# Attention scores from two 12-bit parts in the two halves of the array's rows, in a block of attention and routed experts

## The reference, cut to what matters

```python
def attn(x, Wq, Wk, Wv):                      # x (8, 512, 128), 16 heads of 8 columns; Wk, Wv (8, 128): one k and v for all heads
    q = (x @ Wq.T).reshape(B, S, NH, DK).transpose(0, 2, 1, 3)
    k, v = x @ Wk.T, x @ Wv.T
    dist = softmax(einsum('bhqd,bkd->bhqk', q, k) * DK ** -0.5)
    return einsum('bhqk,bkd->bhqd', dist, v).transpose(0, 2, 1, 3).reshape(B, S, 128)

mod = (silu(c) @ wmod)                         # six rows of 128 for each batch: sa, ca, ga, sb, cb, gb
h = layernorm(x) * (1 + ca) + sa
x = x + ga * attn(h, Wq, Wk, Wv)
h = layernorm(x) * (1 + cb) + sb
x = x + gb * ffn(h)                            # 8 experts of 128 -> 512 -> 128 with gelu, the best 2 for each token
```

## Time and profile before

| what | value |
|---|---|
| runs | 617.99, 621.27 and 1950.61 us, median 621.27 |
| span of the profiled execution, first to last instruction | 616.6 us |
| its own time with what lies around the span | not given; the nearest run is 617.99, 1.4 above the span |
| busy share of the span | PE 90%, DVE 81%, ACT 72%, POOL 52% |
| chain that ended last | PE 66%, DVE 17%, ACT 5% |
| granted TensorE clock | 0.977 of 2.4 GHz over the span |

### The profile page before, as it was taken

One profiled execution on the slowest core, in us unless ns is written; L12 is line 12 of the kernel. 1 busy time (PEld: TensorE's weight loads), 2 busy tenths in 40 slices (PEclk: granted clock), 3 DMA queues, 4 the chain that ended last, 5 costly groups with the idle time before them and its releaser, 6 DMA issues.

```text
span 616.6 us, 18921 instructions
## 1 busy us (share of the span) xinstructions
PE 554.9 (90%) x6699; PEld 307.3 (50%) x6699; DVE 496.7 (81%) x1134; ACT 443.5 (72%) x776; POOL 320.6 (52%) x574
## 2 busy tenths in 40 slices
PE   3669999999999999999999999999799999899970
PEld 2222334333443443443343343343289998799970
DVE  5887999898789779789789779888667777656687
ACT  5683588888788778778877877878765555367771
POOL 1623010134456656666667566666326757665670
PEclk9989999999999999999999999999899999899995
DMA  6299400310311220220220140001223223232645
GB/s 190 66 282 343 132 10 10 75 37 8 78 30 29 69 58 21 70 65 18 61 79 16 35 105 17 27 20 29 51 62 95 79 79 100 84 90 65 201 138 175
DMA packets 49868, 49.32 MB, mean 80 GB/s; under 512 B 15616, under 2 KB 44336, under 8 KB 49056
## 3 DMA queue, kind: packets, MB, share of 16 engines
q1 hardware_dynamic: 42256, 36.89, 21.8%
q0 software_dynamic: 4320, 9.38, 4.7%
q10 hardware_dynamic: 3200, 1.84, 1.0%
HBM read 29.40 MB, written 17.10 MB: 75 GB/s over the span
## 4 chain that ended last, share of the span: by engine, by line
PE 66%; DVE 17%; ACT 5%; issue 3%; DMA 3%; POOL 2%; SPq 2%; DVEq 0%; ACTq 0%; POOLq 0%
PE ps L1096 15%; PE ps L1055 14%; PE ps L1086 12%; DVE neg_max L1401 10%; PE ps L1164 10%; PE ps L1175 9%; ACT P L1263 3%; ACT diag L1273 2%; PE ps L1123 1%; DMA k_parts<-parts 1%; PE ps L1138 1%; PE ps L1155 1%; PE ps L1074 1%; POOL h_sorted L810 1%; PE ps L1130 1%
## 5 line engine op out<-in xcount | busy, mean ns | idle before, releaser
L1401 DVE TENSOR_REDUCE neg_max<-ps 128x1 f32<-128x512 f32 x512 | 321.1, 684 | 54.5 <-PE ps L1055 52.2
L1263 ACT ACTIVATE P<-ps,zero 128x1024 f32<-128x1024 f32 x256 | 272.0, 1110 | 72.8 <-PE ps L1086 71.0
L1055 PE MATMUL ps<-K,Q 128*32 128x512 bf16 x2048 | 183.3, 383 | 5.5 <-DVE neg_max L1401 5.1
L1086 PE MATMUL ps<-Q,K 128*32 128x512 bf16 x2048 | 155.9, 381 | 5.5 <-ACT P L1263 5.1
L1096 PE MATMUL ps<-P,V 128*32 128x512 f32 x1024 | 134.1, 598 | 1.2 <-ACT P L1263 1.1
L1055 PEld LDWEIGHTS ps<-K,Q 128*32 128x32 bf16 x2048 | 54.5, 96 | 109.3 <-DVE neg_max L1401 59.8
L1613 POOL DMA_INDIRECT y_rows<-P,to_now x71 | 73.9, 1041 | 62.9 <-DVE P L1453 30.7
L1319 ACT ACTIVATE parts<-ps,parts 128x128 f32<-128x128 f32 x228 | 64.9, 370 | 41.8 <-PE ps L1164 39.5
L1086 PEld LDWEIGHTS ps<-Q,K 128*32 128x32 bf16 x2048 | 52.3, 97 | 75.7 <-issue 29.5
L810 POOL DMA_INDIRECT h_sorted<-diag,slot x64 | 64.7, 1010 | 28.6 <-POOL max_parts L79 13.4
L1164 PE MATMUL ps<-parts 128*128 128x128 f32 x456 | 61.6, 279 | 2.7 <-DVE parts L1441 1.3
(11 more groups left out here) (239 smaller groups left out, 576.5 us busy)
## 6 DMA issues: line engine op xcount, KB each, us to landing
Q<-q_parts SPq DMA_DIRECT2D x24, 384.0 KB
xs<-h_sorted SPq DMA_DIRECT2D x71, 72.0 KB
W<-w_t SPq DMA_DIRECT2D x2, 2048.0 KB, 11.2
q_parts<-parts SPq DMA_DIRECT2D x8, 384.0 KB, 3.5
Q<-y_rows SPq DMA_DIRECT2D x6, 512.0 KB, 4.5
diag<-att_u SPq DMA_DIRECT2D x128, 16.0 KB
Q<-max_parts SPq DMA_DIRECT2D x96, 4.0 KB, 1.9
out<-Q SPq DMA_DIRECT2D x6, 256.0 KB, 2.3
```

What stands on the lines that cost most here:

```text
L1055: ins = eng.matmul(ring_bank(*unit)[QUAD * q:QUAD * (q + 1), :], Q[buffer_of(g)][:, g % NG * G + j, at:at + QUAD], K[buffer_of(g)][:, 0, : ...
L1086: ins = eng.matmul(bank(2 * u + j)[QUAD * q:QUAD * (q + 1), :], K[p][:, 1, at:at + QUAD], Q[p][:, g % NG * G + 2 * u + j, :], start=True, ...
L1263: nc.scalar.activation(P[s % 2][:, 2 * u:2 * u + 2, :], bank(2 * u, 2).rearrange("p (j t) -> p j t", j=2), ACT.Exp, bias=zero[:], scale=SC ...
L1401: eng.tensor_reduce(neg_max[g % 2][:, j * T + s:j * T + s + 1], ring_bank("maximum", g, s, j), AX.X, ALU.max, negate=True).then_inc(ring_u ...
```

## The change

- Queries, keys and maxima become two parts instead of three. [...] The second part is written by one subtraction, so DVE's first subtraction (L412), ACT's `mid` (L370) and two of POOL's four operations of `split` go.
- `Q[p]` is [128, 8, 512] float32: even heads stand in rows 0 to 63, odd heads in rows 64 to 127. Each half has 32 rows of products, 2 shift rows and 30 rows of zeros.
- A `maximum` is one matmul of 64 rows by 128 columns of weights, in half j % 2. A `scores` is two such matmuls, odd head first. `values` stays as it is.
- Eight sets of buffers for the parts (four of them in `W1`, the values' columns in `W2`), so no batch waits for a store, but the loads of `W1` and `W2` wait for all stores.
- ACT no longer clears `Q`. POOL sets the zeros and ones of `Q` and `K` in twelve chained memsets behind that of `rw`, ahead of the six operations for `mod_T`.
- `load_operands` has 4 DMAs for Q, 8 for K, 1 for V; in the loop 7 of the 13 are issued ahead of the `shift`, which has 4 DMAs instead of 3. The stores and loads carry float32.
- `first` and `res` of the final stage move from `Q` to `diag`.

The core of the diff:

```diff
+HALF, PRODUCTS = 64, 4 * DK
+OPERANDS = HALF
-def split_in_three(own, whole, rest, part):
-    own.link(own.eng.tensor_copy(part[0], whole))
-    own.link(own.eng.tensor_tensor(rest, whole, part[0], ALU.subtract))
-    own.link(own.eng.tensor_copy(part[1], rest))
-    own.link(own.eng.tensor_tensor(part[2], rest, part[1], ALU.subtract))
+def rounded(a):
+    return a.bitcast(F32R)
+def split_in_two(own, whole, part):
+    own.link(own.eng.tensor_copy(rounded(part[0]), whole))
+    own.link(own.eng.tensor_tensor(rounded(part[1]), whole, part[0], ALU.subtract))
...
-        Q = [sb(f"Q{p}", [128, NH, S], BF16) for p in (0, 1)]
-        K = [sb(f"K{p}", [128, 2, S], BF16) for p in (0, 1)]
+        Q = [sb(f"Q{p}", [128, NH // 2, S]) for p in (0, 1)]
+        K = [sb(f"K{p}", [128, 2, S]) for p in (0, 1)]
...
+        def load_operands(eng, b, p, loaded, halves=(0, 1)):
+            for r in halves:
+                for i in (0, 1):
+                    at = HALF * r + 2 * DK * i
+                    eng.dma_start(Q[p][at:at + 2 * DK, :, :].rearrange("p h t -> p (h t)"),
+                                  q_parts[b, i, r].rearrange("d h t -> d (h t)")[:, None, :].to_broadcast([DK, 2, NH // 2 * S])
                                   ).then_inc(loaded[p], 16)
+                    for n in (0, 1):
+                        eng.dma_start(K[p][at:at + 2 * DK, n, :].rearrange("p (q t) -> p q t", q=T),
+                                      k_parts[b].rearrange("(q c) i t -> c i q t", q=T)[KEYS].rearrange("c i q t -> (c i) q t")
+                                      ).then_inc(loaded[p], 16)
+            if 0 in halves:
                 eng.dma_start(V[p][:].rearrange("p t c -> p (t c)"), v_cols[b]).then_inc(loaded[p], 16)
...
         def prepare_gpsimd(eng):
-            for operand in (rw, K[0], K[1]):
-                eng.memset(operand[:].bitcast(I32), 0).then_inc(op_set, 1)
+            own = Chain(eng, op_set)
+            own.link(eng.memset(rw[:].bitcast(I32), 0))
+            for p in (0, 1):
+                for r in (0, 1):
+                    own.link(eng.memset(K[p][other_rows(r), :, :], 0.0))
+                    own.link(eng.memset(K[p][shift_place(r), 1, :], 1.0))
+                    own.link(eng.memset(Q[p][other_rows(r), :, :], 0.0))
             eng.wait_ge(mod_out, START + 1)
...
                 for order, n in enumerate(IN_TURN):
                     eng.wait_ge(hi_done, START + b * 2 + order + 1)
-                    eng.tensor_tensor(rest_of(b, n), projected(b, n), part(b, n, 0), ALU.subtract).then_inc(rest_done, 1)
+                    eng.tensor_tensor(rounded(part(b, n, 1)), projected(b, n), part(b, n, 0), ALU.subtract).then_inc(lo_done, 1)
-                eng.wait_ge(stored[k], START + b // SETS * STORES)
-                for order, n in enumerate(IN_TURN):
-                    eng.wait_ge(mid_done, START + b * 2 + order + 1)
-                    eng.tensor_tensor(part(b, n, 2), rest_of(b, n), part(b, n, 1), ALU.subtract).then_inc(lo_done, 1)
...
-                    for blk in range(3):
-                        at = QUAD * blk + 24
-                        eng.dma_start(Q[buffer_of(g)][at:at + 1, heads_of(g), :], max_parts[g % 2][:, blk, :]).then_inc(shift_loaded[g % 2], 16)
+                    for r in (0, 1):
+                        for part in (0, 1):
+                            at = HALF * r + PRODUCTS + part
+                            eng.dma_start(Q[buffer_of(g)][at:at + 1, pairs_of(g), :], max_parts[g % 2][8 * r:8 * r + 8, part, :]
+                                          ).then_inc(shift_loaded[g % 2], 16)
...
-                    for q in range(128 // QUAD):
-                        at = 128 * s + QUAD * q
-                        ins = eng.matmul(ring_bank(*unit)[QUAD * q:QUAD * (q + 1), :], Q[buffer_of(g)][:, g % NG * G + j, at:at + QUAD],
-                                         K[buffer_of(g)][:, 0, :], start=True, stop=True, tile_position=(0, QUAD * q))
-                    ins.then_inc(ring_full, 1)
+                    p, r = buffer_of(g), j % 2
+                    eng.matmul(ring_bank(*unit), operand(Q[p], r)[:, g % NG * 2 + j // 2, 128 * s:128 * (s + 1)], operand(K[p], r)[:, 0, :],
+                               start=True, stop=True, tile_position=(HALF * r, 0)).then_inc(ring_full, 1)
...
-                    for j in range(2):
-                        for q in range(128 // QUAD):
-                            at = 128 * s + QUAD * q
-                            ins = eng.matmul(bank(2 * u + j)[QUAD * q:QUAD * (q + 1), :], K[p][:, 1, at:at + QUAD],
-                                             Q[p][:, g % NG * G + 2 * u + j, :], start=True, stop=True, tile_position=(0, QUAD * q))
+                    for r in (1, 0):
+                        ins = eng.matmul(bank(2 * u + r), operand(K[p], r)[:, 1, 128 * s:128 * (s + 1)], operand(Q[p], r)[:, g % NG * 2 + u, :],
+                                         start=True, stop=True, tile_position=(HALF * r, 0))
                     ins.then_inc(score_done, 1)
```

More of the change, by code:

```diff
@@ L7 @@
 FP32 = mybir.dt.float32
-BF16 = mybir.dt.bfloat16
+F32R = mybir.dt.float32r
 I32 = mybir.dt.int32
@@ L305, in prepare_sync @@
                 store(eng, b)
+            for b in range(B):
+                eng.wait_ge(stored[b], START + STORES)
             eng.dma_start(W1[:, :, 0:F], w1_t).then_inc(experts_loaded, 16)
@@ L337, in prepare_gpsimd @@
                                   ALU.mult).then_inc(diag_done, 1)
-        def quarters_of(operand, quarters):
-            words = operand[:].bitcast(FP32).rearrange("p h t -> p (h t)")
-            return [words[:, n * NH * S // 8:(n + 1) * NH * S // 8] for n in quarters]
         def prepare_scalar(eng):
-            def clear(p, quarters):
-                for part in quarters_of(Q[p], quarters):
-                    nc.scalar.activation(part, zero[:].to_broadcast(list(part.shape)), ACT.Copy).then_inc(cleared, 1)
             def deviations(tiles):
```

159 lines of the change are left out of this document (66 added, 93 removed).

## The result

The changed kernel takes 654.44 us (median of 4 runs, 650.74 to 655.32), 1.0555 [1.0509, 1.0601] times the kernel before, which ran at 617.99 and 621.27 beside it; two more of its runs, 689.30 and 1950.61 us, are outliers and not in the ratio. It is slower by 5.5%, where 626 was forecast. Its profiled span is 653.0 us against 616.6, so 36.4 us have to be found.

A forecast was written before the change was run, and what follows sets the result against it. PE was taken to set the loop step, DVE 7% behind. Preparation +12.5, loop -8, late shift +3 and end -1 gave +6.5 on 616.6, a span of 623; forecast time 626 us (624.5 to 628), outer range 608 to 660.

The forecast's parts named there:

- The preparation, +12.5: Before the loop: POOL's twelve memsets delay the first `modulate` by 15.5 us; 3 are saved, so the first maximum comes +12.5 us.
- the ends: Start and end of the preparation: no wait for first stores, fewer operations on the last batch, statistics ready; 3 us saved.
- The first shift: First groups: no term given; the prediction only had the `W1` and `W2` loads start near 61 us, needed at 439.
- The ring's cycle, 2.45 to 2.56: Loop step: three banks' cycle of 2.25 us plus 0.20 for shape changes and 0 to 0.107 for a weight load.
- With both loads of the step exposed, 2.66: Loop step: its length in us if neither weight load hides behind a wait.
- its worst case for a batch, 49.5: Four groups of a later batch: 49.5 us with every load exposed, against 47.1 to 48.1 forecast.
- -8: Whole loop, 5 plain groups and 6.25 batches: 8 us saved, taken from -12 to -4; ends -31 and +6.
- Overlap and one pass: Maxima and scores: a 512-column `float32r` matmul streams once in 0.216 us and the two row halves run beside each other.
- The rival that halves don't overlap: Loop step on PE 2.79 us, +25 on 120 steps in place of -8, 656 span, 658; chance 0.16.
- The late shift, +3: Loop refills: more DMAs ahead of the shift overrun its slack by 1 us, six times; +3 us (0 to +8).
- The clock: Rival in the loop: PE streams 69% of a step, the clock halves, a step is 3.6 us, +120; chance 0.04.
- The end, -1: End of the loop and experts: one split fewer ahead of the last batch's chain, -1 us; experts' 167 us unchanged.

The follow-up runs named there:

- e3_clears: Kernel after, with ACT clearing `Q` as before the change and each `K` cleared by one 128-row memset, leaving POOL seven memsets: 643.14 us, 1.0385.
- e2_w_late: Kernel after, with the loads of `W1` and `W2` issued behind `shift(0)` and batch 1's operands: 667.75 us, 1.0783.
- e10_spread: Kernel after, with each loop shift ahead of all refill DMAs, ACT clearing `Q`, seven POOL memsets, weight loads in the third and fourth group: 642.78 us, 1.0365.
- e7_square: Kernel before, with each maximum and score as one bfloat16 matmul of 128x128 in place of four of 128x32: 632.78 us, 1.0215.
- e8_bf16: Kernel after, with maxima and scores reading the upper halves of the words as bfloat16, lower bits left out: 641.78 us, 1.0352.
- e5_order: Kernel after, with the scores' pair in the other order, rows 0 to 63 first: 654.81 us, 1.0571.
- e15_one_half: Kernel after, with all maxima and scores read from rows 0 to 63, odd heads' products left out: two runs, 811.31 and 953.88 us.
- e12_repeat: e10_spread with every pair of score matmuls issued twice over the same bank, same result: 643.11 us, 1.0396.

## Why the prediction was wrong, step by step

The sum was +6.5 and the span grew by 36.4, 30 us more. By size the steps that failed are the ring's cycle with its weight load (14 us), the first shift (8.7, put at nothing) and the clock (6.4, put at nothing); the rest is small.

- *The preparation, +12.5.* Right in mechanism, and in size partly by luck: +12.1. POOL was through with its memsets at 27.38 (27.7 forecast), a memset of 32x4096 took 3.51 as reckoned, rows save nothing (0.94 us for 32x1024, 0.95 in e3_clears for 128x1024). But `modulate` waits for the first of the six operations alone, so it started at 27.79, 13.3 later and not 15.5: the releaser in the earlier trace rows, L323, was only the last event before it, and the section on the kernel before has it wrong too. Against that, 3.4 us at half clock from 37.3 stretched one batch from 2.93 to 4.30 us, and the ends gave about 2.6 instead of 3. 13.3 + 1.4 - 2.6 = 12.1.
- *The first shift.* A term that the prediction put at nothing: +8.7 us in the first two groups. It said that the loads of `W1` and `W2` "start near 61 instead of 45.7 and are needed at 439" and stopped there. It didn't ask what is queued behind them: `shift(0)`, on whose four DMAs of 4 KB the first `scores` waits. e2_w_late confirms the weight loads as cause by moving the wait one group on, and e10_spread takes 6.1 of the 8.7 away. How much of the rest of those two groups is the 13.7 us at half clock from 78.3 on wasn't measured.
- *The ring's cycle, 2.45 to 2.56.* The right cycle with one term too small, and the largest miss. Measured, 2.71. By terms against the 2.25 of before: the fourth maximum to `values` 0.43 instead of 0.216 (115.24 to 115.67), `values` 0.99 instead of 0.86, the first maximum full after 0.50 instead of 0.39. Of these 0.45 the switches are 0.22 (e7_square; 0.20 forecast) and the longer `float32r` loads 0.2 (e8_bf16 takes 0.20 away). The prediction gave the load 0 to 0.107 once; it costs 0.10 at both places where a maximum waits. Its own line "With both loads of the step exposed, 2.66" would have been right within 0.05, and so would its worst case for a batch, 49.5. Over the loop: plain groups 11.18 instead of 10.4 to 10.7, a batch's four groups without late shift 11.62 + 12.51 + 12.73 + 12.65 = 49.5 instead of 47.1 to 48.1. So -8 became about +6 (3 x 0.4 and 6 x 0.8), which the prediction had named as its far end.
- *Overlap and one pass.* Right: pairs every 0.23 to 0.24. That one pass is enough was argued from the width of the parts, which no run shows; what the runs show is that `float32r` pairs keep the pace of bfloat16 ones (e8_bf16). Nor are equal starts the proof that the prediction took them for (e5_order); the pace over several matmuls is. The rival that halves don't overlap (656 span) gives a time close to the measured 653.0, and by the time alone it would have been believed; the trace and e15_one_half (3.06 a step) exclude it. The range up to 660 was opened for this rival, so it is luck that 654.4 lies inside. (2.79 is 0.19 over the present 2.60, not 0.21.)
- *The late shift, +3.* Right: 0.4 to 0.7 us in each of six batches. But the first refill was worse than the others, +2.3 in two groups.
- *The clock.* A rival of 0.04, priced as all or nothing at +120. The true form is small: stretches of 6.8 us at 1.2 GHz, 6.4 us in the loop. The row quoted against it, 20 to 40 us busy 13.5 of 20 at full clock, was from another kind of work and didn't carry over. e12_repeat shows that more matmuls in the same step take the stretches away.
- *The end, -1.* Measured -2.5. The kernel before has 3.4 us at half clock there (from 438.1) and the kernel after none; such a stretch cost 1.1 us in e10_spread's loop.
- *The sum.* 12.1 + 8.7 + 1.2 + 2.3 + 14.7 - 2.5 = 36.5, of which the 14.7 are about 4.8 ring, 3.3 late shift and 6.4 clock. 6.5 had been forecast.

## What to carry to other kernels

When a wait is lengthened on a DMA queue, list what is issued behind it and who waits for that: here four DMAs of 4 KB stood behind 4.6 MB, and taking these away gave back 6.1 of 8.7 us. In a ring of buffers a matmul that waits exposes its weight load as well as its stream, so count the load once for each wait in the cycle, and a change of tile shape once for each turn. And freeing an engine that is the bound is worth only what the next cycle leaves: here four matmul times of PE, 0.8 us a step, were taken away, and a cycle of 2.71 us stood where PE's 2.60 had been.

## What the runs showed of the hardware

- A weight load of 64 rows by 128 columns takes 189 ns in `float32r` and 95 ns in bfloat16, while the moving side of 512 columns costs the same in both (a pair each 0.23 to 0.24 us).
- In bfloat16 a load of 32 columns takes 96 ns (kernel before) and one of 128 columns 98 (e7_square); in float32 109 and 194.
- Going from square tiles to column groups of 32 costs 0.09 us and the way back 0.13, in bfloat16 with full rows (e7_square). The loads don't run ahead of their matmuls at these turns; elsewhere they start 0.21 us ahead.
- Records of matmuls in the same half can start 7 ns apart (e5_order), so equal starts alone don't prove overlap; the pace over several matmuls does.
- The granted clock fell to 1.2 GHz for 157 us with PE's records covering 155.95 of them, when all matmuls but `values` used 64 rows, one at a time (e15_one_half). With pairs it fell, behind the third turn, for 3.4 or 6.8 us at a time, with the scores' pairs issued twice not at all between 75 us and the end of the loop. A busy PE in the records is thus no promise of full clock. What exactly it answers to stays open.
- A POOL memset of 4096 words a row takes 3.51 us over 32 rows; one of 1024 words takes 0.94 over 32 rows and 0.95 over 128 (e3_clears).
